# AdaLN block on one Trainium2 core: the modulation vectors computed as plain float32 products in four 32-column strips, loads and vector work reordered

## What is computed

```
mod = (silu(c) @ wmod).reshape(4, 6, 1, 512)      # c is 4x512, wmod 512x3072
sa, ca, ga, sb, cb, gb = mod[:, 0], ..., mod[:, 5]
ga = sign(ga) * max(|ga|, 0.25); gb likewise
h = layernorm(x) * (1 + ca) + sa
x = x + ga * attention(h)        # 16 heads that share their scores (rank 64), values Wv, output Wo
h = layernorm(x) * (1 + cb) + sb
x = x + gb * ((h @ sum of 8 factors) / sqrt(8) + bias)
```

## Time and profile before

| | us |
|---|---|
| median of 3 runs | 456.58 |
| lowest, highest | 455.72, 457.03 |
| span of the profiled execution | 455.6 |
| PE busy | 447.5 (98%) |
| DVE, ACT, POOL busy | 370.8, 335.6, 235.3 |

### The profile page before, as it was taken

How to read it: one execution, slowest core, us unless ns; L and a number is a source line. 1 busy time by engine, 2 the same in 40 slices (tenths; PEclk the granted TensorE clock), 3 DMA queues, 4 the chain that set the end, 5 groups by cost and what they waited for, 6 DMA issues and landing times.

```text
span 455.6 us, 7390 instructions
## 1 busy us (share of the span) xinstructions
PE 447.5 (98%) x2116; PEld 366.6 (80%) x2116; DVE 370.8 (81%) x643; ACT 335.6 (74%) x673; POOL 235.3 (52%) x306
## 2 busy tenths in 40 slices
PE   9999999999999999999999999999999999999996
PEld 7678788888888788788787888888788888887885
DVE  5898888688777888788778888887887867999977
ACT  5799777677878697886778787886868564767761
POOL 0647445252555534556464645555554527168882
PEclk9999999999999999999999999999999999999999
DMA  8999999533678356768687366849687136758423
GB/s 292 370 318 259 198 179 179 127 90 121 182 223 239 118 161 199 239 184 235 186 228 235 114 202 191 245 135 263 192 230 231 39 125 192 225 162 277 125 85 138
DMA packets 79304, 88.07 MB, mean 193 GB/s; under 512 B 5016, under 2 KB 55960, under 8 KB 79264
## 3 DMA queue, kind: packets, MB, share of 16 engines
q1 hardware_dynamic: 75168, 79.99, 57.7%
q0 software_dynamic: 3808, 7.34, 9.5%
q10 hardware_dynamic: 288, 0.27, 0.2%
HBM read 53.49 MB, written 34.10 MB: 192 GB/s over the span
## 4 chain that ended last, share of the span: by engine, by line
PE 52%; DMA 21%; DVE 11%; ACT 5%; issue 5%; POOL 4%; SPq 3%; POOLq 0%; DVEq 0%; ACTq 0%
DMA x_blocks<-xn 10%; DMA xb<-x_blocks 7%; PE ps_o L537 6%; PE ps_o L539 6%; PE ps_o L538 6%; PE ps_v L537 4%; PE ps_v L538 4%; PE ps_v L539 4%; DVE negmax L1291 3%; PE ps_y L537 2%; PE ps_y L539 2%; PE ps_qk L537 2%; PE ps_y L538 2%; PE ps_t L543 2%; PE ps_qk L538 2%
## 5 line engine op out<-in xcount | busy, mean ns | idle before, releaser
L1746 POOL TENSOR_SCALAR ve<-mv 128x1 f32<-128x1 f32 x64 | 20.9, 327 | 152.1 <-DVE mv L1347 118.0
L539 PE MATMUL ps_o<-v_hi,pt_hi 128*128 128x512 f32 x192 | 74.7, 389 | 0.0
L537 PE MATMUL ps_o<-v_lo,pt_hi 128*128 128x512 f32 x192 | 74.7, 389 | 0.0
L538 PE MATMUL ps_o<-v_hi,pt_lo 128*128 128x512 f32 x192 | 74.7, 389 | 0.0
L872 ACT ACTIVATE h_f<-x1b,mod_t 128x128 f32<-128x128 f32 x120 | 53.1, 597 | 8.1 <-DVE x1b L1365 8.0
L872 ACT ACTIVATE h_f<-xb,mod_t 128x128 f32<-128x128 f32 x80 | 35.5, 593 | 20.2 <-DVE xb L1361 20.0
L1232 DVE TENSOR_TENSOR h_lo<-h_f,h_hi 128x512 fp32r<-128x512 f32 x57 | 41.4, 726 | 9.5 <-ACT h_hi L844 9.3
L1748 POOL TENSOR_TENSOR rstd<-ve,minus_half 128x1 f32<-128x1 f32 x64 | 42.7, 667 | 5.3
L537 PE MATMUL ps_v<-wvo_lo,h_hi 128*128 128x512 f32 x112 | 44.4, 396 | 0.0
L538 PE MATMUL ps_v<-wvo_hi,h_lo 128*128 128x512 f32 x112 | 43.8, 391 | 0.0
L539 PE MATMUL ps_v<-wvo_hi,h_hi 128*128 128x512 f32 x112 | 43.6, 389 | 0.0
(11 more groups left out here) (236 smaller groups left out, 1238.1 us busy)
## 6 DMA issues: line engine op xcount, KB each, us to landing
x_blocks<-xn SPq DMA_DIRECT2D x50, 256.0 KB, 3.0
p_blocks<-probs SPq DMA_DIRECT2D x24, 512.0 KB, 3.5
pb<-p_blocks SPq DMA_DIRECT2D x96, 128.0 KB, 3.2
x1b<-x_blocks SPq DMA_DIRECT2D x30, 256.0 KB, 2.9
result<-x_ring SPq DMA_DIRECT2D x15, 512.0 KB, 2.9
f_sum<-in_factors POOLq DMA_DIRECT2D x14, 512.0 KB, 6.2
xb<-x_blocks SPq DMA_DIRECT2D x20, 256.0 KB, 2.9
x_ring<-in_x SPq DMA_DIRECT2D x18, 256.0 KB, 3.4
```

Of the source, the lines that this page charges most:

```text
L537: nc.tensor.matmul(acc, a_hi, b_lo, start=first, stop=False)
L538: nc.tensor.matmul(acc, a_lo, b_hi, start=False, stop=False)
L539: return nc.tensor.matmul(acc, a_hi, b_hi, start=False, stop=last)
L1746: nc.gpsimd.tensor_scalar(ve[:, one], mv[:, u, 1:2], EPS, None, ALU.add).then_inc(ve_done, 1)
```

## The change

- The parts of wmod, the 36-column stationary matrix, the low rows and their additions are gone. silu(c) stays float32 (128x4 for a chunk) and is multiplied with wmod as it was loaded.
- Each chunk k is four products, one in each strip of 32 columns of the array; strip j writes rows 32j to 32j+3 of one PSUM bank. `first_vectors` makes SA and CA: four strips of 256 columns, 16 products, after the wvo terms of chunk 1. `other_vectors` makes GA, GB, SB, CB: four strips of 512 columns, 8 products in `prep_pair(2)` and 8 in `prep_pair(3)`.
- The whole bank is copied out and turned by full 128x128 transposes: 2 in `first_columns`, 4 in `other_columns`. Both gates are bounded at once.
- SP loads both first chunks of Wv and Wo ahead of wmod, and the rest of wmod in four loads of 1 MB that wait for no product.
- All four `wv_rest` are on DVE. DVE's and ACT's lists are reordered: `moments_of(0)` and `x_row(0)` come earlier, `h_of(1)` and the parts of tile 1 between the parts of wvo, and `moments_of(8)` stands behind the values of tile 4.

The core of the diff:

```diff
             load_v_and_o(0)
+            load_v_and_o(1)
             load_wmod(0)
             load_wmod(1)
-            load_v_and_o(1)
+            load_first_x(0, x_first)
             load_wmod(2)
             load_wmod(3)
-            load_first_x(0, x_first)
             load_v_and_o(2)
...
             load_x(1)
-            sp.wait_ge(mod_acc, CA + 1)
-            load_vector(GA)
-            load_vector(SB)
+            load_rest(0)
             load_x(2)
+            load_rest(1)
             sp.dma_start(f_sum[:], factors[0].rearrange("(c p) n -> p c n", p=P)).then_inc(f0_loaded, 16)
-            load_vector(CB)
             load_x(3)
+            load_rest(2)
+            load_rest(3)
             load_x(4)
-            load_vector(GB)
             load_x(5)
...
+            def first_vectors():
+
+                pe.wait_ge(silu_steps, 3)
+                pe.wait_ge(bank_cleared, 1)
+                half = D // 2
                 for k in range(C):
-                    vector_part(v, k, w_lo, k == 0, False)
-                    last = vector_part(v, k, w_hi, False, k == C - 1)
+                    pe.wait_ge(wmod_loaded[k], 16)
+                    for j in range(4):
+                        last = nc.tensor.matmul(ps_s[STRIP * j:STRIP * j + B, 0:half], silu_c[:, k, :],
+                                                wmod_0[:, k, half * j:half * (j + 1)], start=k == 0, stop=k == C - 1)
                 last.then_inc(mod_acc, 1)
...
+            def other_vectors(chunks):
+
+                for k in chunks:
+                    pe.wait_ge(rest_loaded[k], 16)
+                    for j, v in enumerate(STRIPS):
+                        last = nc.tensor.matmul(ps_y[STRIP * j:STRIP * j + B, :], silu_c[:, k, :],
+                                                wmod_1[:, k, rest_columns(v)], start=k == 0, stop=k == C - 1)
+                if k == C - 1:
+                    last.then_inc(mod_acc, 1)
...
             weights_term(0, 0, 1)
-            pe.wait_ge(silu_steps, 6)
-            early_upper(0)
-            early_rest(0)
-            early_upper(1)
-            early_rest(1)
             weights_term(1, 0, 0)
             weights_term(1, 1, 0)
-            early_upper(2)
-            early_rest(2)
-            early_upper(3)
-            early_rest(3)
             weights_term(1, 0, 1)
+            first_vectors()
             weights_term(2, 0, 0)
             weights_term(2, 1, 0)
-            pe.wait_ge(ident_set, 2)
-            pe.wait_ge(rows_done, 2)
-            modulation_columns(0, (SA, CA))
+            first_columns()
             weights_term(2, 0, 1)
             transpose_x(0)
             weights_last(3)
             prep_pair(0)
-            prep_pair(1, lambda: modulation(GA))
-            prep_pair(2)
-            prep_pair(3, lambda: modulation(SB), third_vector)
-            pe.wait_ge(rows_done, ROW_READ[CB])
-            modulation_columns(1, (SB, CB))
+            prep_pair(1)
+            prep_pair(2, lambda: other_vectors((0, 1)))
+            prep_pair(3, None, first_scores)
+            other_columns()
...
             step(0, transpose_first_late)
-            step(1, transpose_second_late, last_vector)
+            step(1, transpose_second_late, lambda: pe.wait_ge(h_f_done, TB + 3))
```

More of the change, by code:

```diff
@@ L16 @@
 WARMUPS = 8
[L17 removed]
+STRIP = 32
 Q = 4
 BLK = P // Q
[L20 to L21 removed]
+STRIPS = (GA, GB, SB, CB)
 LAST_EARLY = 4
@@ L183, in adaln_block @@
         probs = sb("probs", [P, KEYS])
[L184 to L187, removed]
+        early = P + 4 * B
+        zeros = probs[:, 0:early]
+        rows_1, rows_2, signs = pb[:, 1, 0:D // 2], pb[:, 0, 0:D], pb[0:STRIP + B, 1, D:2 * D]
         ps_s = bank("ps_s", KEYS)
@@ L231, in adaln_block @@
         weights_hi_done, weights_lo_done = sem("weights_hi_done"), sem("weights_lo_done")
[L232 to L235, removed]
+        bank_cleared = sem("bank_cleared")
         mod_acc = sem("mod_acc")
-        rows_done = sem("rows_done")
+        rows_copied = sem("rows_copied")
+        gate_steps = sem("gate_steps")
         mod_tps = sem("mod_tps")
@@ L292, in turned_probs, with rest_columns @@
             return pb[:, trips_of(t) & 1, :].rearrange("p (b k c) -> p k b c", b=Q, c=BLK)
[L294 to L302, removed]
+        def rest_columns(v):
+            return slice(D * (v - GA), D * (v - GA + 1))
         late = TILES - PER_BATCH
@@ L580, in transpose_x, with first_columns, other_columns @@
+            def first_columns():
+                pe.wait_ge(ident_set, 2)
+                pe.wait_ge(rows_copied, 1)
+                transposes(mod_t_banks[0], rows_1, 2).then_inc(mod_tps, 1)
+            def other_columns():
+                pe.wait_ge(rows_copied, 2)
+                transposes(mod_t_banks[1], rows_2, C).then_inc(mod_tps, 1)
             def transpose_x(q, acc=ps_t[1], rows=xn):
@@ L1150, in _ @@
             values_of(6)
-            low_row(CB)
             exponentials(0)
+            copy_rows()
             values_of(7)
-            step(0, beside=lambda: [vector_upper(GB, k) for k in range(C)])
-            step(1, behind=lambda: low_row(GB))
+            step(0)
+            step(1)
             act.wait_ge(mod_t_done, 4)
@@ L1499, in _ @@
             nc.vector.memset(minus_half[:], -0.5).then_inc(consts_set, 1)
-            nc.vector.memset(no_parts, 0.0).then_inc(consts_set, 1)
-            rows = [0]
-            def row(v):
-                dve.wait_ge(mod_acc, v + 1)
-                dve.wait_ge(low_copied, v + 1)
-                wait(dve, rows_done, rows[0])
-                nc.vector.tensor_tensor(mod_row(row_of[v]), mod_banks[v][0:B, :], mod_row(low_of[v]),
-                                        ALU.add).then_inc(rows_done, 1)
-                rows[0] += 1
@@ L1533, in columns, with other_columns @@
                                             ALU.add).then_inc(mod_t_done, 1)
-            def last_vector_rests():
-                for k in range(C):
-                    vector_rest(GB, k)
+            def other_columns():
+                dve.wait_ge(mod_tps, 2)
+                turned = mod_t_banks[1][:].rearrange("p (c j r) -> p j c r", c=C, r=STRIP)
+                for i in range(2):
+                    nc.vector.tensor_scalar(mod_t[:, :, 2 + i, :].rearrange("p b c -> p c b"),
+                                            turned[:, 2 + i, :, 0:B], float(i), None,
+                                            ALU.add).then_inc(mod_t_done, 1)
@@ L1627, in _ @@
             h_second(8)
-            row(CB)
             values_of(6)
             values_of(7)
-            columns(1)
-            step(0, last_vector_rests, lambda: bound_gate(GA))
+            other_columns()
+            step(0, None, bound_gates)
             dve.wait_ge(bias_loaded, 16)
-            step(1, lambda: row(GB))
-            step(2, lambda: bound_gate(GB))
+            step(1)
+            step(2)
             for t in range(3, T - TB):
```

263 lines of the change are left out of this document (78 added, 185 removed).

## The result

The changed kernel takes 459.76 us, the median of 20 runs (456.47 to 465.83), against 455.44 for the kernel before in 20 runs (453.95 to 458.56): ratio 1.0081, 95% interval 1.0058 to 1.0103. It is slower by 0.6 to 1.0%. The forecast was 459.0, range 454.2 to 463.0.

A forecast was written before the change was run, and what follows sets the result against it. PE, busy 98% of the span, was taken as the bound. Late adds move tile 10 from 74.67 to 79.0, less 1.9 in step 1: +2.4 on 455.6 gives 458.0, plus 1.0 for the median, 459.0; range 454.2 to 463.0.

The forecast's parts named there:

- Removed work: PE's list: six vectors of products (11.6 us) and two sets of small transposes (1.2) go, together 12.8 us.
- The strips, taken pairwise: Modulation products on PE: only neighbouring strips overlap, by one record, so 11.3 us, between bounds of 5.6 and 22.6.
- the third rival: Modulation and step 1: all four strips run together (5.6 us) and adds don't bind, span 454.4; chance 0.13.
- Waits up to tile 2: Prologue on PE: first values at 23.3 as before, then a 1.5 us wait; tile 2's transposes at 27.7.
- PE's own flow to tile 10: Prologue to step 1: PE's list and waits, without the adds, reach tile 10's transposes 3.8 us later, at 78.5.
- The rival with all four strips: Prologue to step 1: strips all together take 5.6 us, so PE's flow reaches tile 10 at 74.4; chance 0.13 or 0.20.
- the copy of the rows: Prologue, ACT copying the bank behind tile 0's exponentials: 0.7 us of wait allowed, bounds 0 and 1.2.
- The chain of adds: POOL's factor adds, begun late behind tile 8's moments: 3a at 54.6, 6b at 73.6 to 75.1, tile 10's transposes at 79.0.
- all together and the adds bind: Step 1: strips take 5.6 us, adds hold tile 10 until 76.6, span 456.6, no change; chance 0.20.
- likeliest case: Whole kernel: strips overlap pairwise and adds hold tile 10; 459.0 us, own range 457.3 to 462, chance 0.52.
- products that fill 4 columns: Strip products on PE: TensorE's clock might fall beside them, one reason for up to 3 us more.
- 1.9 of GB: Step 1 on PE: GB's products are gone from there, worth 1.9 us less.

The follow-up runs named there:

- one_strip: Changed kernel with all 32 plain products of the modulation on strip 0, summed into the same rows; median 469.25 us, ratio 1.0295 to the kernel before.
- strips_in_turn: Changed kernel with the same products ordered strip by strip instead of chunk by chunk; ratio 1.0097 to the kernel before.
- before_moments8_late: Kernel before with only the moments of tile 8 moved on DVE behind the values of tile 4; ratio 1.0064 to the kernel before.
- m8_and_wvo: Changed kernel with moments of tile 8 early again and wvo parts 2 and 3 ahead of h_of(1); median 456.80 us, ratio 1.0004 to the kernel before.

## Why the prediction came out

The time came out (459.0 for 459.76), and the main reason, late adds at tile 10, was right. That the number fits so well is in part luck. It was built as a change of +2.4 on a median that the three first runs had put at 456.58; the kernel before takes 455.44 in 20 runs, and the change is 3.7 by the ratio. So the base was 1.1 too high and the change 1.3 too small. Inside the change one large term was wrong, and the hold at tile 10 hid it.

- **Removed work, 12.8 us:** nothing measured speaks against it.
- **The strips, taken pairwise at 11.3: wrong.** The step "the second record must wait for the first, and PE starts its products in the order of its list; then only the second record of one strip and the first of the next can overlap" failed. Measured: 1.9 for the first block, 1.83 and 1.90 for the halves, 5.6 in all, the third rival's 5.6. Four records start at once, the next four 0.43 later. Up to 41.50 the timeline has

```profile
41.22 0.61 PE L536 MATMUL ps_y<-wmod,silu_c 128*4 128x512 f32 x4
```

so the first record of the fourth product starts ahead of the second record of the first, against the order of the list. one_strip shows that it is the strips, strips_in_turn that two products in a row on one strip don't even matter. The change to the strips and back cost about as little as taken (43.05 to 43.39 is 0.34, where the usual step is 0.23). The rule of the Trainium skill (TensorE: Matmul & The Clock Gate, Part 3: Packing small matmuls) that column groups run concurrently is borne out, with 3.8 for four strips; its rule that products keep their order in start and end, on which I hung the pairwise half, does not hold for these records.
- **Waits up to tile 2:** close. First values at 23.75 for 23.3, the gap 1.25 for 1.5, tile 2's transposes 28.10 for 27.7. Missed: 0.65 for the first part of wvo, and 1.39 for the third chunk of Wv, which a short first block lays bare.
- **PE's own flow to tile 10, 78.5: wrong by the strips' size,** and less wrong than these: it came at 79.44 - 3.07 = 76.4. The rival with all four strips had 74.4. Of the 2.0 between, 0.8 had gathered by tile 2's transposes (28.10, where the rival has 27.3) through the waits above, and 0.82 is the wait at tile 8 for xn(8). The remaining 0.4 I have not followed; the copy of the rows is no part of it, with a wait of 0.31 where 0.7 was allowed.
- **The chain of adds: right, with two errors that cancel.** Add 3a at 54.15 for 54.6, 6b at 75.87 for 73.6 to 75.1 (6.8 an add from 3b on, not 6.4), tile 10's transposes at 79.44 for 79.0. 6b came 0.8 later than the latest forecast, and from it to the transposes took 3.6 instead of 4.5: in the kernel before POOL took 2.3 from the end of 6b to nmr(10), here 1.4. (The lower end, 73.6, does not follow from the 5.5 an add that stands beside it; that gives 72.4.) From 3b on the chain runs on the transfers and not on PE, and PE began the values of tile 4 only 1.5 earlier than forecast (43.05 for 44.5), so the strips' error hardly reached it: before_moments8_late gets the same hold without any strip. The rival "all together and the adds bind" had the mechanism that happened, and 76.6 for it, because it let the adds follow PE by 2.3 us; 3a came 0.5 earlier.
- **Not in the sum:** the gates, which would have held tile 10 at 78.6 by themselves (SP's and the DMAs' part of step 1 was costed at nothing), and the fall of the clock behind the wait, 2.8. (The likeliest case's own lower end, 457.3, is 1.7 below 459.0, where the text names 1.0.) The range had a clock in it, but for products that fill 4 columns, and that did not happen.

So to step 3: +1.7 flow + 3.1 hold + 2.8 clock - 1.9 of GB = +5.7, which is 102.64 - 96.94. The profiled span is only 3.9 longer; the 1.8 between lies within the 6 us by which that stretch differs among executions, and no cause for it is shown. The wider spread of the changed kernel's runs (9.4 us for 4.6) comes from the clock at most in part. Averaged over a run, the granted clock of the 20 is 0.994 in the mean, against 0.999 over 80 later executions of the kernel before, and it is lowest, 0.983, in the slowest run (465.83); but a run of 460.68 had 1.000.

## What to carry to other kernels

Work taken off the bound engine is worth only what its suppliers can follow: here 12.8 - 5.6 - 0.6 (the full transposes) = 6.6 us of TensorE's work went, and the waits up to tile 10 rose from 0.2 to 8.3 us. Before an instruction is moved down a list, look who stands behind its result; two short moments on DVE stood ahead of a series of transfers that wait for one another, and that is where the time went. And price a new wait with the clock behind it: 3.1 us of idle cost 5.9 in the changed kernel and 4.7 in before_moments8_late.

## What the runs showed of the hardware

- Four strips of 32 columns run plain float32 products 3.8 times as fast as one (1.83 for 6.96 us, 8 products of 512 columns), also with two products in a row on each strip (1.85), but not with four in a row (4.43 for 1.9, 16 products of 256). There the first four records start singly, then two together.
- TensorE's clock fell to 0.50 in or behind waits of 1.91, 3.06, 3.07, 3.09 and 3.33 us in step 1 and one of 2.39 in the prologue, and was at full level behind waits of 0.83, 1.18, 1.63, 1.78 and 1.82. Behind the wait of 1.4 for the third chunk it fell in one profile and stayed in six. The low level lasted 6.8 us in two of these falls (cost 2.8) and 3.4 in the others (cost 1.6 to 1.8 where it was measured).
- The 256 KB of the first gate took 4.0 to 6.3 us from issue to landing in 13 profiles and 7.0 in m8_and_wvo's, beside adding DMAs, though the lists around it were nearly the same.
